# Filler work between score blocks, exchanged expert halves, an early reload and a residual added by TensorE in a vision tower on one core

## What is computed

```python
h = einsum('bnk,dk->bnd', patches, W)                  # D = 192
q, k, v = silu(h @ Wq), silu(h @ Wk), silu(h @ Wv)     # 12 heads of 16
energy = einsum('bhnd,bhmd->bhnm', q, k) * decay       # decay: exp(slope * (n - m)), 0 above the diagonal
a = einsum('bhnm,bhmd->bhnd', energy, v) * sigmoid(h @ Wg1 @ Wg2)
h = layernorm(h + layernorm(a @ Wo) * ln_w + ln_b)
xn = rms_norm(h) * norm_w
logits = einsum('sd,btd->bst', l2(slots) * scale, l2(xn))   # 64 slots
y = einsum('btd,bst->bsd', xn, softmax(logits, tokens))
y = gelu(einsum('sio,bsi->bso', fc1, y) + fc1_bias)         # each slot has its own 192 x 768
y = einsum('sio,bsi->bso', fc2, y) + fc2_bias               # and its own 768 x 192
h = layernorm(h + einsum('bsd,bst->btd', y, softmax(logits, slots)))
```

## Time and profile before

| | us |
|---|---|
| median of 3 runs | 1350.14 (1349.92 to 1350.39) |
| the profiled execution | 1349.98 |
| its span on the core | 1348.2 |
| image passes | to about 1021 |
| expert steps | 1022.5 to 1239.7 |
| seam and output stage | 1239.7 to 1348.2 |

### The profile page before, as it was taken

The page is one execution under the profiler, slowest core; times in us unless marked ns, Lnnn a source line. Parts: engine busy times, 40 slices in busy tenths (PEclk is TensorE's granted clock), DMA queues, the critical chain, the costliest instruction groups (busy, mean ns, idle before and its releaser), DMA issues.

```text
span 1348.2 us, 34010 instructions
## 1 busy us (share of the span) xinstructions
PE 1219.4 (90%) x12578; PEld 972.2 (72%) x12578; DVE 784.1 (58%) x2049; ACT 711.3 (53%) x1613; POOL 565.2 (42%) x846
## 2 busy tenths in 40 slices
PE   5999999999999999999999999999978999997563
PEld 4788888888888888888888888888854555554332
DVE  4666666666666666666666666666661111111797
ACT  5456666666665666666666566666642111110466
POOL 5254455444555445544455544554430000000564
PEclk8999999999999999999999999999987999999555
DMA  4412111111112111111111211111162999993886
GB/s 154 159 62 70 51 48 48 48 48 48 48 48 72 68 51 48 48 48 48 48 48 48 72 68 51 48 48 57 74 235 89 367 367 373 367 352 92 233 262 190
DMA packets 50708, 158.33 MB, mean 117 GB/s; under 512 B 5370, under 2 KB 31344, under 8 KB 38384
## 3 DMA queue, kind: packets, MB, share of 16 engines
q1 hardware_dynamic: 33072, 145.04, 30.9%
q10 hardware_dynamic: 17600, 12.78, 3.1%
HBM read 132.18 MB, written 25.62 MB: 117 GB/s over the span
## 4 chain that ended last, share of the span: by engine, by line
PE 79%; DVE 15%; issue 1%; DMA 1%; ACT 1%; SPq 1%; DVEq 1%; POOL 0%; ACTq 0%; POOLq 0%
PE ps L908 9%; PE ps L909 8%; PE ps L910 8%; DVE p_sb L773 7%; PE ps L967 7%; PE ps L938 6%; PE ps L1002 6%; PE ps L1166 5%; PE ps L1182 4%; PE ps L1186 4%; PE ps L1045 3%; PE ps L950 3%; PE ps L951 2%; PE ps L985 2%; PE ps L1068 2%; PE ps L1195 2%
## 5 line engine op out<-in xcount | busy, mean ns | idle before, releaser
L409 POOL TENSOR_TENSOR xl<-x_sb,xh 128x392 fp32r<-128x392 f32 x192 | 190.1, 1031 | 211.6 <-DVE gn L748 203.2
L773 DVE TENSOR_TENSOR p_sb<-ps,dec 98x1176 f32<-98x1176 f32 x128 | 176.9, 1382 | 84.4 <-PE ps L967 84.4
L967 PE MATMUL ps<-qm,kT 32*98 32x196 f32 x1536 | 117.0, 343 | 39.0 <-DVE p_sb L773 39.0
L967 PEld LDWEIGHTS ps<-qm,kT 32*98 32x98 f32 x1536 | 75.2, 158 | 70.4 <-DVE p_sb L773 58.3
L631 ACT ACTIVATE hg<-ps 128x768 f32<-128x768 f32 x32 | 25.9, 811 | 184.8 <-PE ps L1186 184.8
L712 DVE BATCH_NORM_STATS2 st<-ps 98x6 f32<-98x192 f32 x128 | 40.1, 355 | 129.9 <-PE ps L938 129.9
L1002 PE MATMUL ps<-p_sb,vpad 98*32 98x98 f32 x3072 | 112.4, 250 | 0.8 <-DVE p_sb L773 0.8
L1002 PEld LDWEIGHTS ps<-p_sb,vpad 98*32 98x32 f32 x3072 | 84.5, 109 | 34.3 <-issue 33.0
L873 DVE COPY y2st<-ps 128x192 f32<-128x192 f32 x32 | 11.5, 358 | 155.7 <-PE ps L1166 155.7
L938 PE MATMUL ps<-wo,og 96*98 96x192 f32 x512 | 93.7, 325 | 0.0
L496 POOL CAST pickb<-pick 128x128 fp32r (+1 forms) x32 | 9.4, 294 | 192.1 <-PE ps L1186 192.1
(11 more groups left out here) (174 smaller groups left out, 3379.9 us busy)
## 6 DMA issues: line engine op xcount, KB each, us to landing
x_sb<-in_xT SPq DMA_DIRECT2D x32, 1176.0 KB, 5.7
w1v<-in_fc SPq DMA_DIRECT2D x32, 1152.0 KB, 7.6
w2v<-in_fc SPq DMA_DIRECT2D x32, 1152.0 KB, 9.9
...
```

The lines of the kernel that those rows point to most:

```text
L409: pool.tensor_tensor(xl[:, k], x_sb[:, k], xh[:, k].bitcast(F32), ALU.subtract)\
L773: dve.tensor_tensor(dst, src, rate.unsqueeze(2).to_broadcast([T, PAIRS, 2, TOK]), ALU.mult)\
L967: mm = pe.matmul(ps[0:T, SC_AT + r, mt * TOK:(mt + 1) * TOK].rearrange("p (b n) -> p b n", b=2), kT[rows, g, n], qm[rows, g, :, n], start= ...
```

## The change

It has four parts.

- **Image passes.** On PE `logits_turned` goes from before the keys to behind the gate, ahead of the second block of scores, and `carried(0)` and `carried(1)` go ahead of the fourth block. On DVE `slot_maxima` goes behind `kts`, and `gated(0)` before decay 3. On POOL `qd` goes ahead of `split_x`.
- **Exchanged halves.** In the second half x of fc1 slot 0 writes to the rows of slot 1 and the other way round, for which the bias has a third copy of the slot selector; the four matmuls over the last 64 inputs now stand together. fc2 picks its columns accordingly. `y2st` has three buffers.
- **Early reload.** `cbuf` and `h2r` have a place of their own, and are loaded for the first four pairs right after the last weights. y2 is reloaded in three pieces of whole rows: of 26 steps, of four, of the last two. POOL waits for all of it once.
- **Residual.** For the first image of a pair (banks 2n) PE adds the residual itself, with a matmul of the identity by `h2r`; DVE takes its statistics from PSUM, and ACT reads it from PSUM. DVE adds the residual for the second image only. The bank is now free only when ACT has read it.

The diff, cut to its core:

```diff
...
@@ -144,12 +148,14 @@
             w2v.append(place(f"w2v{n}", [128, 2, FJ, D]))
 
 
-        place = placer(region_at)
+        slot_at = [region_at + 4 * (2 * F + Y2 * D + n * SLOT) for n in range(EARLY)]
+        place = placer(slot_at[REST])
         y2r = place("y2r", [128, NP, D])
-        place = placer(region_at + 4 * (2 * F + 2 * D) + REST * 4 * (3 * F + 2 * FJ * D))
+        place = placer(slot_at[EARLY - 1] + 4 * SLOT)
         cbuf, h2r = place("cbuf", [128, DEEP, TOK]), place("h2r", [T, DEEP, 4, D])
+        place = placer(region_at + STAGE_AT)
         y2b = place("y2b", [128, DEEP, D])
-        res, o_sb = place("res", [T, DEEP, 4, D]), place("o_sb", [T, DEEP, 4, D])
+        res, o_sb = place("res", [T, DEEP, 2, D]), place("o_sb", [T, DEEP, 4, D])
 
 
         og = sb("og", [G, 2, PT])
@@ -357,20 +363,18 @@
                     slot_step(RING * v + n, n)
             for n in range(REST):
                 slot_step(RING * (TURNS - 1) + n, n)
-            sp.wait_ge(fc2_mm, RING * TURNS)
-
-
             sp.wait_ge(h2_stored, 16 * NP)
             sp.wait_ge(comb_stored, 16 * NP)
             for n in range(DEEP):
                 load_comb(n, n)
                 load_h2(n, n)
-            for par in range(2):
-                sp.wait_ge(y2_stored[par], 16 * NU // 2)
-            for n in range(DEEP):
-                c = slice(n * NP // DEEP, (n + 1) * NP // DEEP)
+            sp.wait_ge(fc2_mm, RING * TURNS - 2)
+            for u0, u1 in zip((0,) + READY[:-1], READY):
+                for m in range(Y2):
+                    sp.wait_ge(y2_stored[m], 16 * ((u1 - m + Y2 - 1) // Y2))
                 for a in range(2):
-                    sp.dma_start(y2r[64 * a:64 * a + 64, c, :], y2_dram[:, a, c, :]).then_inc(y2r_loaded[n], 16)
+                    rows = slice(64 * a + 2 * u0, 64 * a + 2 * u1)
+                    sp.dma_start(y2r[rows, :, :], y2_dram[2 * u0:2 * u1, a]).then_inc(y2r_loaded, 16)
             with sp.Fori(0, NP // DEEP - 1) as w:
                 for n in range(DEEP):
                     p = DEEP * w + n
...
@@ -493,7 +497,10 @@
                 if not (isinstance(u, int) and u < 2):
                     pool.wait_ge(fc1_mm, u - 1)
                 src = pick[:, :].rearrange("p (u s) -> p u s", s=2)
-                pool.tensor_copy(pickb[:, n % 2], src[:, u].unsqueeze(2).to_broadcast([128, 2, NB])).then_inc(pick_rdy, 1)
+                pool.tensor_copy(pickb[:, n % 2, 0:2], src[:, u].unsqueeze(2).to_broadcast([128, 2, NB]))\
+                    .then_inc(pick_rdy, 1)
+                pool.tensor_copy(pickb[:, n % 2, 2:3], src[:, u, 0:1].unsqueeze(2).to_broadcast([128, 1, NB]))\
+                    .then_inc(pick_rdy, 1)
             phase2(pool, slot_step)
 
             def out_rstd(p, n):
...
@@ -645,7 +650,8 @@
                 if not at_start(w):
                     act.wait_ge(out_stored[n], 16 * w)
                 for t in range(4):
-                    act.activation(o_sb[:, n, t], res[:, n, t], ACT.Identity,
+                    src = ps[0:T, 2 * n, t * D:(t + 1) * D] if t < 2 else res[0:T, n, t - 2]
+                    act.activation(o_sb[:, n, t], src, ACT.Identity,
                                    bias=nb3[:, n, t:t + 1], scale=rstd3[:, n, t:t + 1]).then_inc(o_rdy, 1)
                 act.wait_ge(o_rdy, 4 * p + 4)
                 act.dma_start(out_v[p], o_sb[:, n]).then_inc(out_stored[n], 16)
...
@@ -844,6 +850,8 @@
                                       ps[0:T, 5, 0:2 * D].rearrange("p (a h d) -> p a h d", a=2, h=H),
                                       kdec[:, :].unsqueeze(1).unsqueeze(3).to_broadcast([T, 2, H, HD]),
                                       ALU.mult).then_inc(kts_rdy, 1)
+                    if d:
+                        slot_maxima(i - 2)
                     decay(i, 1)
                     dve.wait_ge(s_mm, i + 1)
                     dve.tensor_tensor(state[:, :, :].rearrange("p x (h d) -> p x h d", h=HG),
@@ -854,23 +862,22 @@
                     sums(i - 2)
                 if a:
                     decay(i, 2)
-                if a:
+                    gated(i, 0)
                     decay(i, 3)
-                    gated(i, 0)
                     gated(i, 1)
             phase1(dve, step)
 
 
             def slot_step(u, n, v):
-                par = n % 2
+                m = n % Y2
                 dve.wait_ge(tr_mm, u + 1)
                 dve.tensor_copy(hgT[:, :, :].rearrange("p (x j) b -> p x (j b)", x=2), ps[:, 2:4, 0:FH])\
                     .then_inc(hgT_rdy, 1)
-                if not (isinstance(u, int) and u < 2):
-
-                    dve.wait_ge(y2_stored[par], 16 * (RING // 2 * v + n // 2))
+                if not (isinstance(u, int) and u < Y2):
+
+                    dve.wait_ge(y2_stored[m], 16 * (RING // Y2 * v + n // Y2))
                 dve.wait_ge(fc2_mm, u + 1)
-                dve.tensor_copy(y2st[:, par], ps[:, 4 + par, 0:D]).then_inc(y2st_rdy, 1)
+                dve.tensor_copy(y2st[:, m], ps[:, 4 + n % 2, 0:D]).then_inc(y2st_rdy, 1)
             phase2(dve, slot_step)
 
             def out_step(p, n, w):
@@ -878,13 +885,13 @@
                 dve.wait_ge(h2r_loaded[n], 16 * w + 16)
                 if not at_start(w):
                     dve.wait_ge(o_rdy, 4 * (p + 1 - DEEP))
-                dve.tensor_tensor(res[0:T, n].rearrange("p (x t) d -> p x (t d)", x=2),
-                                  ps[0:T, 2 * n:2 * n + 2, 0:2 * D],
-                                  h2r[:, n].rearrange("p (x t) d -> p x (t d)", x=2), ALU.add)\
-                    .then_inc(res_rdy, 1)
+                dve.tensor_tensor(res[0:T, n].rearrange("p t d -> p (t d)"), ps[0:T, 2 * n + 1, 0:2 * D],
+                                  h2r[:, n, 2:4].rearrange("p t d -> p (t d)"), ALU.add).then_inc(res_rdy, 1)
+                for t in range(2):
+                    dve.bn_stats(st3[:, n, t, :], ps[0:T, 2 * n, t * D:(t + 1) * D])
                 dve.wait_ge(res_rdy, p + 1)
-                for t in range(4):
-                    dve.bn_stats(st3[:, n, t, :], res[0:T, n, t])
+                for t in range(2):
+                    dve.bn_stats(st3[:, n, 2 + t, :], res[0:T, n, t])
                 dve.drain()
                 for t in range(4):
                     dve.bn_aggr(mv3[:, n, t, :], st3[:, n, t, :]).then_inc(mv3_rdy, 1)
@@ -1118,7 +1125,7 @@
                                          hTh[:, k, n], hTl[:, k, n], wvh[:, k], wvl[:, k], k == 0, k == 1)
                         if t % 2:
                             mm.then_inc(v_mm, 1)
-                if d:
+                if d and not a:
                     logits_turned(i - 2)
                 if a:
                     for g in range(2):
@@ -1130,6 +1137,8 @@
                     scores(i, 0, c)
                     keys_turned(i)
                     gate(i)
+                    if d:
+                        logits_turned(i - 2)
                     scores(i, 1, c)
                     values(i, 0)
                     states(i)
@@ -1140,10 +1149,10 @@
                         pe.wait_ge(g_sb, 2 * i + 2)
                     dispatch_turned(i - 2)
                 if a:
+                    carried(i, 0)
+                    carried(i, 1)
                     scores(i, 3, c)
                     values(i, 2)
-                    carried(i, 0)
-                    carried(i, 1)
                 if d:
                     slot_inputs(i - 2)
                 if a:
@@ -1156,6 +1165,9 @@
             phase1(pe, step)
             pe.wait_ge(cb_sb, NP)
             pe.wait_ge(yT_sb, 2 * NP)
+
+            def half_of(s, x):
+                return s if x == 0 else 1 - s
 
             def fc2_pair(u, n):
                 pe.wait_ge(hgT_rdy, u + 1)
@@ -1163,27 +1175,30 @@
                     pe.wait_ge(y2st_rdy, u - 1)
                 for k in range(FJ):
                     for s in range(2):
-                        mm = pe.matmul(ps[64 * s:64 * s + 64, 4 + n % 2, 0:D], hgT[:, k, 64 * s:64 * s + 64],
+                        at = 64 * half_of(s, k // 3)
+                        mm = pe.matmul(ps[64 * s:64 * s + 64, 4 + n % 2, 0:D], hgT[:, k, at:at + 64],
                                        w2v[n][:, s, k], start=(k == 0), stop=(k == FJ - 1))
                 mm.then_inc(fc2_mm, 1)
 
             def slot_step(u, n, v):
                 start = isinstance(u, int) and u == 0
                 pe.wait_ge(w_loaded[n], 32 * v + 32)
-                pe.wait_ge(pick_rdy, u + 1)
+                pe.wait_ge(pick_rdy, 2 * u + 2)
                 if not start:
                     pe.wait_ge(gelu_rdy, u)
                 y_u = yT0[:, :, :].rearrange("p (u s) b -> p u s b", s=2)
                 for x in range(2):
                     f = slice(x * FH, (x + 1) * FH)
-                    pe.matmul(ps[:, x, 0:FH], pickb[:, n % 2].rearrange("p s b -> p (s b)"), bias1[:, f],
```

(23 more changed lines are left out.)

34 lines of the change are left out of this document (18 added, 16 removed).

## The result

The changed kernel takes 1306.59 us (median of four runs, 1303.82 to 1311.00), the kernel before 1350.03 beside it (1349.29 to 1350.39): a ratio of 0.9682, 95% interval 0.9654 to 0.971, or 43 us less. The forecast was 1291, its range 1278 to 1312. So the sign and the range held and the centre was 15.6 us too low. The profiled execution took 1305.92, with a span of 1304.2; its gains, against the span of 1348.2, are read from three marks: the first gelu of the experts, the end of the last fc2 and the end of the span.

A forecast was written before the change was run, and what follows sets the result against it. PE was taken to set the image passes, PE and nearly full DMA the experts, DVE the output stage. Gains 28.5 + 24 + 1.7 + 5.0 = 59.2 off 1348.2 gave 1289.0, plus 1.9: 1291; range 1278 to 1312.

The forecast's parts named there:

- at most 0.1 is lost there: Image pass: keys of the second half wait for zs of DVE, ready just as they would start; loss at most 0.1 us.
- the first move: Image pass: the L1053 matmuls go from between values and keys to behind the gate; 0.58 us off the path.
- The second move: Image pass: carried goes from behind values(2) to before the fourth scores; 0.40 of 0.45 us can be had.
- Both covers on DVE: Image pass: lneg (0.36 us) hides in a DVE wait of 0.56, gated(0) (0.55) in one of 1.03.
- rival B: Image pass: one wait comes back, for zs, qd or lt; gain 13 instead of 28.5, 1306 us; chance 0.12.
- rival A: Experts: the four quadrants run two by two; gain 2.5 instead of 24, 1308 us; chance 0.14.
- The weights come at 98% of the DMA engines: Experts: DMA needs 6.50 us per pair of experts and ends 1.4 us later than PE would want; gain 24.
- The bound of 5.8 us per pair of experts: Experts: DMA's lower bound, weights at 410 GB/s, where PE decides and the gain is 25.6 us.
- 7.0 - 5.3 = 1.7: Seam: pair 0 at 13.8 us behind fc2, less two more periods of 2.66 to do; gain 1.7 us.
- DVE waits for no store here: Experts: the third y2st buffer costs nothing, as DVE does not wait for stores.
- Rival C: Output stage: it stays at 1.2 GHz and PE sets 2.86 us per pair; 1302 us; chance 0.08.
- Rival D: Output stage: the ring of loads decides, h2r being asked for only after res; slower, 1355 us at a 13.6 landing; chance 0.03.

The follow-up runs named there:

- run 1: The kernel before with the image-pass moves alone: 1328.29 us, ratio 0.9839.
- run 5: The changed kernel with ACT copying zs before it makes qm and qs of the second half of the heads: 1297.24 us, ratio 0.9604.
- run 2: The kernel before with the exchanged halves of fc1 and fc2 alone, third cast on POOL included: 1325.32 us, ratio 0.9823.
- run 4: The changed kernel with the reload of y2 behind the last store, in four pieces by pairs: 1303.58 us, ratio 0.9662.
- run 7: The changed kernel with the reload's last 6 expert pairs behind the last store, in four pieces by image pairs: 1298.03 us, ratio 0.9612.
- run 8: The changed kernel with the output stores issued by SP, two pairs behind, and not by ACT: 1291.30 us, ratio 0.9572.

## Why the prediction was right, and what was off

**Image pass: right place, mis-sized, 0.98 us a pass where 0.68 was measured (22.3 us for 28.5 in the stretch, 21.1 in run 1).** The step that failed is "at most 0.1 is lost there". In the trace of before zs ran from 487.45 to 488.02, and the keys, drawn 0.58 earlier to 486.94, reach their second half after six steps of 0.18, at 488.02 as well. PE then starts 0.26 behind the end of zs (508.82 to 509.08). I had left out the price of the handing over. The rows of before:

```profile
487.45 0.57 DVE L834 TENSOR_TENSOR zs<-ps,zs 16x392 fp32r<-16x392 f32 x1 [0.95 <-ACT zs L566]
```

```profile
489.83 0.91 PE L967 MATMUL ps<-qm,kT 32*98 32x196 f32 x12
```

The second row is the first block of scores, up to which the first move is measured in run 5. Run 5 removes the wait and gets 0.32 a pass back, so the 0.58 itself was sound. The second move was taken at 0.40 and gave 0.34. Both covers on DVE held, and rival B (a whole wait back, 13 of 28.5) did not come in full: 6.2 of its 15.5 us did.

**Experts: the number right, a reason wrong.** Four quadrants run together, so rival A is out. The forecast took 25.6 off PE and gave 1.4 back to DMA. Run 2 has neither: 31 steps by 0.78 make 24.2. "The weights come at 98% of the DMA engines" was read as a limit (2.46 MB of weights and store in 6.50 us are 378 GB/s); the same engines then carried 422 at a share of 1.02. The bound of 5.8 us per pair of experts, from the 410 GB/s of the earlier trace rows, was the sound one. In the changed kernel 0.7 of the 24.2 went to the wait for a store.

The Trainium skill (TensorEngine Tiling, Gotcha 1) has different row tiles kept from one PSUM bank at a time. Eight records of L1201 take what four of L1186 took (0.81 and 0.80 us to the next row), and tiles of both row halves write into each of the two banks: for different partitions of a bank the trace does not agree.

**The seam: sign wrong.** The forecast was 7.0 - 5.3 = 1.7. In its terms pair 0 at 16.7 against pair 2 at 20.8 makes 4.1 - 5.3 = -1.2, and the wait for the store, counted with the experts above, costs another 0.7. The prediction's own sign, that it is wrong if the seam grows, came. Two steps failed. "DVE waits for no store here": a store takes 1.7 to 2.5 us with no reload beside it (run 4) and 18.2 with it, longer than three buffers cover at 5.85 us a step. And the landing was computed from bytes over a rate, 11.4 behind fc2, where 14.3 was measured: the last pieces cannot be issued before the last store has landed (1200.2, 5.8 us after its issue at 1194.4), and then run on few engines. Run 4 shows that the early reload gains nothing as it is made. Cut by pairs, so that POOL waits for a quarter of the tail, it does gain: run 7 is 8.6 us faster than the changed kernel (4.9 of it at pair 0 in the profiled executions) and 5.6 faster than the late reload of run 4, with intervals that do not meet.

The Trainium skill (DMA: Bandwidth & Descriptors, on why a DMA increments its semaphore by 16) gives a load of 4 rows 4 engines. The trace agrees: the packets of those loads go four at a time, and the share is 0.23 to 0.26. The prediction had set that rule aside with 3 us as its price, and pair 0 came 2.9 late. That the two are so near is luck: the 5.8 us of the last store, which the prediction did not have, are part of the 14.3 as well.

**Output stage: 2.5 forecast, 2.65 measured.** The 31 periods take 82.2 us. Eleven of them, 34.7 us, stand at 1.2 GHz with 2.97 us and more, the other twenty at 2.4 GHz or on the way between. PE's price at 1.2 GHz was mis-sized, 2.86 for 3.07. At 2.4 GHz the steady pace is 2.54, not 2.42: ACT's reads from PSUM and SBUF hardly differ (0.91 and 0.97 for two), so ACT's pace of before, 2.53, stayed. DVE had come down to 2.07, which the stage used for no more than a few pairs after each rise of the clock (run 8 uses it throughout). So the half of the residual took the bound from DVE and gave it to ACT at the one clock and to PE at the other: that is where this part's gain went. Rival C held for eleven pairs, not for all. PE waited for ACT 15 times, 12.5 us in all, where the prediction had this wait just covered (9.7 us in four periods). Rival D did not appear.

With the 1 us more that the last pairs take to leave ACT, the sum reads 28.5 - 6.2, 24 - 0.5, and 6.7 - 8.5: 59.2 less 15.2 is 44.0, the difference of the two spans. Every term missed to the same side; the range held because it took in the bounds and the rivals, not because the centre was near.

The changed kernel's spread of 7 us goes with the clock: the four runs have a mean granted clock of 0.973, 0.964, 0.960 and 0.956, and 1303.8, 1305.9, 1307.3 and 1311.0 us.
